# MLA layer: norm weights folded into the weight casts, and the norm epilogue issued one pass later

## The reference

```python
q_a  = x @ q_a_w.T                                  # 1536 wide
q    = rmsnorm(q_a, q_a_ln_w) @ q_b_w.T             # 16 heads of 128 + 64
ckv_full = x @ kv_a_w.T                             # 512 + 64 wide
kv   = rmsnorm(ckv_full[..., :512], kv_a_ln_w) @ kv_b_w.T
# rotary embedding on the 64-wide parts, causal attention over 2048 keys, attn @ o_w.T
x = layernorm(x + attention)
x = layernorm(x + (silu((x @ gate_w.T) * gate_s) * ((x @ up_w.T) * up_s)) @ down_w.T * down_s)

def rmsnorm(x, w):
    var = mean(x * x, -1);  return w * (x * rsqrt(var + 1e-6))
```

## Time and profile before

| | us |
|---|---|
| two runs | 5514.85 and 5719.79, median 5617.32 |
| profiled execution | 5525.08 |
| its span, slowest core (core 0) | 5523.5 |
| the eight cores' spans | 5457.2 to 5523.5 |
| busy: TensorE, VectorE, ScalarE | 3832.7, 1938.4, 1574.5 |

### The profile page before, as it was taken

One profiled execution on the slowest core, in us unless ns is written; L12 is line 12 of the kernel. 1 busy time (PEld: TensorE's weight loads), 2 busy tenths in 40 slices (PEclk: granted clock), 3 DMA queues, 4 the chain that ended last, 5 costly groups with the idle time before them and its releaser, 6 DMA issues.

```text
span 5523.5 us, 67067 instructions; the slowest of 8 cores (5457.2 to 5523.5 us)
## 1 busy us (share of the span) xinstructions
PE 3832.7 (69%) x20050; PEld 1841.4 (33%) x20400; DVE 1938.4 (35%) x4074; ACT 1574.5 (29%) x3152; POOL 327.9 (6%) x581
## 2 busy tenths in 40 slices
PE   0466657666666666666365679885998599859986
PEld 0222323223333333333122234342434244424443
DVE  2333222544444444444223233323332333233323
ACT  0000000025545454555200033222332233223322
POOL 0000000000000000000000011111111011111111
PEclk9877778878778887788677789997999899989998
DMA  4100022000000000000501079876887588658975
GB/s 127 57 31 31 20 71 67 16 12 9 5 9 5 11 5 9 5 5 1 152 31 38 23 232 279 255 249 196 277 271 244 187 277 281 230 187 268 279 247 183
DMA packets 207570, 674.50 MB, mean 122 GB/s; under 512 B 30016, under 2 KB 30528, under 8 KB 203136
## 3 DMA queue, kind: packets, MB, share of 16 engines
q1 hardware_dynamic: 120816, 341.68, 19.4%
q0 software_dynamic: 78928, 310.68, 18.0%
q10 hardware_dynamic: 7488, 17.83, 1.1%
HBM read 653.05 MB, written 16.78 MB: 121 GB/s over the span
## 4 chain that ended last, share of the span: by engine, by line
PE 35%; DMA 32%; DVE 13%; issue 11%; ACT 8%; DVEq 1%; SPq 0%; ACTq 0%; POOL 0%; POOLq 0%
DMA stg_gp<-up_l 20%; PE pD L1134 6%; PE pPT L556 5%; DMA stg_gp<-down_c 5%; PE pOP L924 4%; PE pQA L417 3%; ACT Ebuf L829 3%; PE pO L778 3%; ACT PTsb L801 3%; DVE ubf L229 2%; PE pPT L794 2%; PE pS L741 2%; DVE stats L759 2%; DMA stage<-ow_l 1%; PE pS L752 1%
## 5 line engine op out<-in xcount | busy, mean ns | idle before, releaser
L1063 PE MATMUL pU<-OX,ubf 128*128 128x512 bf16 x2756 | 644.8, 384 | 131.2 <-DVE ubf L229 127.0
L1054 PE MATMUL pG<-OX,gbf 128*128 128x512 bf16 x2760 | 641.2, 383 | 136.3 <-ACT gbf L226 133.5
L1134 PE MATMUL pD<-h_fm,dbf 128*128 128x512 bf16 x2756 | 625.5, 383 | 83.5 <-DVE dbf L229 75.8
L229 DVE CAST ubf<-stg_gp 128x1024 bf16<-128x1024 f32 x352 | 244.5, 695 | 871.7 <-DMA stg_gp<-up_l 854.9
L778 PE MATMUL pO<-PTsb,vtm 128*128 128x128 bf16 x2176 | 239.0, 238 | 312.3 <-ACT PTsb L801 305.8
L1063 PEld LDWEIGHTS pU<-OX,ubf 128*128 128x128 bf16 x2816 | 269.9, 99 | 496.3 <-issue 201.7
L1054 PEld LDWEIGHTS pG<-OX,gbf 128*128 128x128 bf16 x2816 | 277.5, 99 | 471.4 <-issue 145.7
L1134 PEld LDWEIGHTS pD<-h_fm,dbf 128*128 128x128 bf16 x2816 | 273.3, 99 | 423.3 <-issue 125.2
L801 ACT CAST PTsb<-pPT 128x512 bf16<-128x512 f32 (+3 forms) x640 | 313.5, 524 | 279.3 <-PE pPT L794 277.7
L829 ACT ACTIVATE Ebuf<-pS,stats 128x512 bf16<-128x512 f32 (+3 forms) x512 | 314.3, 621 | 208.7 <-DVE stats L820 207.6
L1076 ACT ACTIVATE sig<-pG,gates_sb 128x512 bf16<-128x512 f32 x176 | 120.9, 687 | 880.7 <-DVE tmid L1081 684.0
(11 more groups left out here) (135 smaller groups left out, 3756.1 us busy)
## 6 DMA issues: line engine op xcount, KB each, us to landing
stg_gp<-up_l POOLq DMA_DIRECT2D x352, 512.0 KB, 6.3
stg_sy<-gate_l SPq DMA_DIRECT2D x352, 512.0 KB, 6.3
stg_sy<-down_c SPq DMA_DIRECT2D x128, 512.0 KB, 6.0
stg_gp<-down_c POOLq DMA_DIRECT2D x128, 512.0 KB, 5.2
stg_sy<-down_c SPq DMA_DIRECT2D x64, 384.0 KB, 7.1
stg_gp<-down_c POOLq DMA_DIRECT2D x64, 384.0 KB, 4.4
stage<-x SPq DMA_DIRECT2D x64, 256.0 KB, 3.0
xst<-x POOLq DMA_DIRECT2D x16, 1024.0 KB, 5.7
```

Of the source, the lines that this page charges most:

```text
L229: e.tensor_copy(d[:, a:a + cc], tiles[i][:, 0:cc]), inc=cP)
L1054: P.op("tensor", lambda e, wi=wi, d=d, gc0=gc0: e.matmul(pG[wi][:], gbf[wi][:, d * 128:(d + 1) * 128], OX[:, d * S + gc0:d * S + gc0 + 512 ...
L1063: P.op("tensor", lambda e, wi=wi, d=d, gc0=gc0: e.matmul(pU[wi][:], ubf[wi][:, d * 128:(d + 1) * 128], OX[:, d * S + gc0:d * S + gc0 + 512 ...
L1134: P.op("tensor", lambda e, di=di, hh=hh, jj=jj, ii=ii: e.matmul(pD[di][:], dbf[hh][:, jj * 128:(jj + 1) * 128], h_fm[:, ii * 512:(ii + 1) ...
```

## The change

1. `qaln_rep` and `kvln_rep` are replaced by `qaln_cols` (128x12) and `kvln_cols` (128x4): column k holds the norm weights of rows 128k to 128k+127 of the weight matrix. The four staged loads and casts go; two small DMAs come, ahead of the tables, into tiles that need no cast.
2. The norm weights are multiplied onto the weights as these are cast. In stage A2 the 36 casts on VectorE become `tensor_scalar_mul` and the 36 on ScalarE become `activation` with function Copy and a scale of one value for each partition. In the heads each of the 32 `kvw3` casts becomes four multiplies of 128x128, as each block has its own column of weights.
3. In the epilogue the two VectorE operations that made `rq_tm` and `ckv_tm` (L448, L466) become Copy activations on ScalarE with the root as scale. Both sums of squares come first, then both means, both reciprocals, both roots, both copies.
4. The epilogue of pass t-1 is emitted in pass t, behind the x transposes and their evictions (L397) and behind the four casts of the next x chunk (L405), and ahead of `emit_a1_tr`. `emit_a1_tr` also waits on TensorE for the two copies.

```diff
-        def cast_stage(slot, ld, dst_ap, cols, eng="vector"):
+        def cast_stage(slot, ld, dst_ap, cols, eng="vector", scale=None):
...
+                P.op(eng, lambda e, i=slot, d=dst_ap, c=cols, s=scale:
+                     e.tensor_scalar_mul(d, stage[i][:, 0:c], s), inc=cW)
...
+                                 e.activation(d[:, a:a + cc], tiles[i][:, 0:cc],
+                                              AF.Copy, scale=sc), inc=cP)
...
+        P.op("sync", lambda e: e.dma_start(out=qln_c[:], in_=qaln_cols_in), inc=dC0, k=16)
+        P.op("sync", lambda e: e.dma_start(out=kln_c[:], in_=kvln_cols_in), inc=dC0, k=16)
...
-                load_cast(qaln_rep, qaln_sb, 0, QL)
-                load_cast(kvln_rep, kvln_sb, 0, LAT)
...
+                def emit_a1_epi(pi, pt, pmm):
+                    nonlocal pqa_free, pckv_free, pkpe_free
+                    P.w("scalar", sAct, sAct.n)
+                    P.w("scalar", tMM, pmm)
+                    P.op("scalar", lambda e: e.activation(
+                        junk[:, 0:QL], pQA[:], AF.Square,
+                        accum_out=stats[:, 0:1]), inc=sAct)
+                    sq_qa = sAct.n
+                    P.op("scalar", lambda e: e.activation(
+                        junk[:, 1536:1536 + LAT], pCKV[:], AF.Square,
+                        accum_out=stats[:, 3:4]), inc=sAct)
+                    sq_ckv = sAct.n
+                    P.w("vector", sAct, sq_qa)
+                    P.op("vector", lambda e: e.tensor_scalar(
+                        stats[:, 1:2], stats[:, 0:1], rql[:], EPS_RMS,
+                        op0=ALU.mult, op1=ALU.add), inc=vStat)
+                    P.w("vector", sAct, sq_ckv)
+                    P.op("vector", lambda e: e.tensor_scalar(
+                        stats[:, 4:5], stats[:, 3:4], 1.0 / LAT, EPS_RMS,
+                        op0=ALU.mult, op1=ALU.add), inc=vStat)
+                    P.w("vector", vStat, vStat.n)
+                    P.op("vector", lambda e: e.reciprocal(stats[:, 1:2], stats[:, 1:2]), inc=vStat)
+                    P.op("vector", lambda e: e.reciprocal(stats[:, 4:5], stats[:, 4:5]), inc=vStat)
+                    P.w("scalar", vStat, vStat.n)
+                    P.op("scalar", lambda e: e.activation(
+                        stats[:, 2:3], stats[:, 1:2], AF.Sqrt), inc=sAct)
+                    P.op("scalar", lambda e: e.activation(
+                        stats[:, 5:6], stats[:, 4:5], AF.Sqrt), inc=sAct)
+                    P.w("scalar", sAct, sAct.n)
+                    P.op("scalar", lambda e, pi=pi: e.activation(
+                        rq_tm[pi][:], pQA[:], AF.Copy,
+                        scale=stats[:, 2:3]), inc=sAct)
+                    pqa_free = (sAct, sAct.n)
+                    P.op("scalar", lambda e, pi=pi: e.activation(
+                        ckv_tm[pi][:], pCKV[:], AF.Copy,
+                        scale=stats[:, 5:6]), inc=sAct)
+                    pckv_free = (sAct, sAct.n)
+                    P.w("vector", dC1, tm_ld)
+                    P.w("vector", tMM, pmm)
+                    P.op("vector", lambda e: e.tensor_copy(kpe_sc[:], pKPE[:]), inc=vE)
+                    pkpe_free = (vE, vE.n)
+                    P.w("vector", vE, vE.n)
+                    P.op("vector", lambda e, pt=pt: e.tensor_mul(
+                        kpe_r1[:], kpe_sc[:], cos_tm[:, pt * ROPE:(pt + 1) * ROPE]), inc=vE)
+                    swap_ap = bass.AP(kpe_sc, 32, [[ROPE, 128], [-32, 2], [1, 32]])
+                    P.op("vector", lambda e, pt=pt, sw=swap_ap: e.tensor_tensor(
+                        kpe_r2[:].rearrange("p (a b) -> p a b", a=2), sw,
+                        sins_tm[:, pt * ROPE:(pt + 1) * ROPE].rearrange("p (a b) -> p a b", a=2),
+                        ALU.mult), inc=vE)
+                    P.w("vector", vE, vE.n)
+                    P.op("vector", lambda e: e.tensor_add(
+                        kpe_bf[:], kpe_r1[:], kpe_r2[:]), inc=vE)
+                    return vE.n
...
                 def emit_a1_tr(pi, pt, pkpe_done):
                     P.w("tensor", vE, pkpe_done)
+                    P.wf("tensor", pqa_free)
+                    P.wf("tensor", pckv_free)
...
                     if pend_epi is not None:
-                        emit_a1_tr(*pend_epi)
+                        kd = emit_a1_epi(*pend_epi)
+                        emit_a1_tr(pend_epi[0], pend_epi[1], kd)
...
-                    kpe_done = vE.n
-                    pend_epi = (i, t, kpe_done)
+                    pend_epi = (i, t, a1_mm)
...
+                            load_cast(src[grp, k], qbw_bf, slots[k] * 512, 512,
+                                      scale=qln_c[:, k:k + 1])
...
+                def kv_load(src, dst):
+                    sl, ld = stage_load(src, LAT)
+                    P.w("vector", dWs[sl], ld)
+                    P.w("vector", dC0, ln_cols_ld)
+                    for l in range(LATC):
+                        P.op("vector", lambda e, sl=sl, dst=dst, l=l: e.tensor_scalar_mul(
+                            dst[:, l * 128:(l + 1) * 128],
+                            stage[sl][:, l * 128:(l + 1) * 128],
+                            kln_c[:, l:l + 1]), inc=cW)
+                    stage_free[sl] = (cW, cW.n)
```

More of the change, by code:

```diff
@@ L181, in stage_load, with load_cast @@
             return i, dWs[i].n
-        def cast_stage(slot, ld, dst_ap, cols, eng="vector"):
+        def cast_stage(slot, ld, dst_ap, cols, eng="vector", scale=None):
             P.w(eng, dWs[slot], ld)
             if eng == "scalar":
-                P.op(eng, lambda e, i=slot, d=dst_ap, c=cols:
-                     e.copy(d, stage[i][:, 0:c]), inc=cS)
+                if scale is None:
+                    P.op(eng, lambda e, i=slot, d=dst_ap, c=cols:
+                         e.copy(d, stage[i][:, 0:c]), inc=cS)
+                else:
+                    P.op(eng, lambda e, i=slot, d=dst_ap, c=cols, s=scale:
+                         e.activation(d, stage[i][:, 0:c], AF.Copy, scale=s), inc=cS)
                 stage_free[slot] = (cS, cS.n)
                 return cS.n
-            P.op(eng, lambda e, i=slot, d=dst_ap, c=cols:
-                 e.tensor_copy(d, stage[i][:, 0:c]), inc=cW)
+            if scale is None:
+                P.op(eng, lambda e, i=slot, d=dst_ap, c=cols:
+                     e.tensor_copy(d, stage[i][:, 0:c]), inc=cW)
+            else:
+                P.op(eng, lambda e, i=slot, d=dst_ap, c=cols, s=scale:
+                     e.tensor_scalar_mul(d, stage[i][:, 0:c], s), inc=cW)
             stage_free[slot] = (cW, cW.n)
             return cW.n
-        def load_cast(src_ap, dst_tile, dst_c0, cols, eng="vector"):
+        def load_cast(src_ap, dst_tile, dst_c0, cols, eng="vector", scale=None):
             done = 0
@@ L201, in load_cast @@
                 done = cast_stage(sl, ld, dst_tile[:, dst_c0 + c0:dst_c0 + c0 + cc],
-                                  cc, eng)
+                                  cc, eng, scale)
                 c0 += cc
@@ L210, in mk_path, with lc @@
             st = {"free": [None] * nslots, "i": 0}
-            def lc(src_ap, dst_tile, dst_c0, cols):
+            def lc(src_ap, dst_tile, dst_c0, cols, scale=None):
                 done = None
@@ L431, in build_program @@
                     x0_free[i] = (tMM, a1_mm)
[L432 to L467, removed]
-                        op0=ALU.mult, op1=ALU.mult), inc=vE)
@@ L541, in q_group @@
                         if k % 2 == 0:
+                            P.w("vector", dC0, ln_cols_ld)
                             P.wf("vector", slot_free[slots[k]])
[L543 removed]
+                            load_cast(src[grp, k], qbw_bf, slots[k] * 512, 512,
+                                      scale=qln_c[:, k:k + 1])
                         else:
+                            P.w("scalar", dC0, ln_cols_ld)
                             P.wf("scalar", slot_free[slots[k]])
[L546 removed]
+                            w_cp = lc_a2(src[grp, k], qbw_bf, slots[k] * 512, 512,
+                                         scale=qln_c[:, k:k + 1])
                     w_ready = cW.n
```

65 lines of the change are left out of this document (29 added, 36 removed).

## The result

| | before | changed |
|---|---|---|
| all runs made side by side, median, us | 5665.25 (15 runs) | 5566.84 (16 runs) |
| lowest | 5510.81 | 5446.07 |
| profiled execution | 5525.08 | 5503.52 |
| ratio, with its 95% interval | | 0.9899 [0.9858, 0.9939] |

The changed kernel is 1.0% faster (0.6 to 1.4%), some 56 us of 5525. The two medians lie some 150 and 90 us above the runs that the ratio compares, because in over half of these executions (10 of 17 of the changed kernel) the cores of one die show a lower granted clock, 0.78 to 0.84 against 0.86, and the ratio leaves those out.

What follows compares the result with a forecast made beforehand. It took VectorE's single queue between products in stage A1, x load's round trip included, as the bound. Terms -38.5 - 1.7 - 6.0 + 1 + 4.8 = -40.4 us from 5525.1 gave 5485 us, range 5450 to 5530.

Steps and rivals of the forecast that it cites:

- the term for the spread between executions: Whole kernel: the slowest core's time alone was said to move by some 10 us between executions; used for the range.
- The gap of a pass: Stage A1, between one product's end and the next one's start: 2.6 us less in 15 gaps, 38.5 us (28 to 42).
- The rebuilt pass: Stage A1: one pass retimed station by station with the change, from product end at 427.24 to next product at 441.9.
- The clock: Stage A1 product: low granted clock in its first 5.3 us; bounds nothing to 37 us gain, counted as nothing.
- rises sooner: Rival in stage A1: TensorE's clock rises earlier in the product; full gain 5448 us, half 5466; chance 0.12.
- The start: Kernel start: tables issued from 2.9 instead of 8.87 us, so all later SyncE work moves 6.0 us earlier.
- Behind the last pass: End of stage A1, with no x load: the epilogue reaches the transposes at 700.3 instead of 701.98, 1.7 us less.
- A2: Stage A2: scaled casts cost 2.2 us more on VectorE, about nothing on ScalarE; +1 us taken (-1 to +3).
- The heads: Heads: four multiplies replace each cast; 16 on the path at 0.3 us each, +4.8 us (0 to 19).
- on which everything of that head waits: Heads: the values' multiplies run directly ahead of the head's first maximum and delay the whole head; 0.3 us each.
- No table was loaded: Rival: ScalarE reloads its function table around the copies; one load on the path 5505 us, both 5526; chances shared with others.
- The gap didn't stay: Rival in stage A1: evictions and squares slow each other, 2.8 us more per pass, 5523 us; 0.05 shared with double table loads.

Runs made afterwards that it cites:

- e3: Changed kernel with one plain 128x512 cast instead of four multiplies for each of the 32 head weights; heads 1457.3 us against 1457.9.
- e1: Kernel before with only the epilogue moved one pass later, behind the x evictions and casts; ratio to the kernel before 0.9949, pass 33.0 us on die 1.
- e2: Changed kernel with the epilogue back behind its own product, all else as changed; ratio 0.9880, pass 30.47 us.
- e4: Changed kernel with the next x chunk's four casts moved behind the evictions of the transposes; ratio 0.9839, pass 27.25 us on six cores.
- e7: Changed kernel with four stage buffers in place of two up to the end of stage A1; one run, 5429.76 us, pass 27.33 us.
- e5: Changed kernel with the epilogue back behind its own product and the x casts behind the transposes' evictions; ratio 0.9756, pass 26.10 us.
- e8: Changed kernel with epilogue back behind its own product, x casts behind the transposes' evictions, and four stage buffers; ratio 0.9712, pass 26.30 us.

## Why the prediction held, and where it failed

I forecast 5485 us, 5450 to 5530, and the median of all runs is 5566.84. **The step that failed is the last one, from the sum to the range: the term for the spread between executions, put at "some 10 us".** The runs showed in its place a spread of 314 us: the sixteen of the changed kernel go from 5446.07 to 5760.32, ten of them above 5530, and the fifteen of the kernel before from 5510.81 to 5825.83. The sum was made against the profiled execution, which lay by the lower of the two runs shown, and these two were 205 us apart already. By the median of the two I had 5577, only 10 us from the result, but that is luck: the median of the kernel before came out 48 us higher with fifteen runs. A range for a median of such runs would have had to reach as far as the 5665 of the kernel before, whatever the change.

The step of 40.4 us that the sum gives stands beside 56 (34 to 78) by the ratio and 43.2 by the two profiles. The seven runs on which the ratio rests, from 5446.07 to 5503.52 (the profiled one), have 5473.62 in the middle. So the sum was sound, in part by luck: its terms for the gap and for the clock were off in opposite directions.

The terms, as far as the profiles part them:

- **The gap of a pass**: forecast 2.6 us, measured 2.3 over the passes (1.8 in the two shown, 16.9 to 15.1). The rebuilt pass met nearly every station: evictions 0.56 behind the transposes (0.54 forecast), 2.60 for them (2.80), statistics 0.69 (0.7), roots 0.38 (0.4), copies and release 2.37 (2.15), to the product 3.77 (3.98, of which 0.4 is the missing record). Only the casts were 4.71 instead of 4.13, with a wait for x of 2.98 instead of 2.43 us. I had taken that wait from a single pass, and a short one: over all cores and passes with an x load the waits come to 3.0 us a pass before, where that pass has 2.6. In the changed kernel they come to 3.25, so that "the wait doesn't shrink" was right and it grew by 0.2.
- **The clock**, counted at nothing, gave the 0.7 us by which the product got shorter; in the two products shown half of 5.3 - 3.7 is 0.8. That is 11 us, and the rival "rises sooner" came true to a third of its bound of 37. With 34.6 by the gaps the passes gave 45.6 us for 38.5.
- **The start**: the tables were issued at 2.92, for 2.9 forecast, which is the whole 6 us on SyncE:

```profile
1.98 0.42 SPq L267 DMA_DIRECT2D qln_c<-qaln_cols  x1
2.45 0.43 SPq L268 DMA_DIRECT2D kln_c<-kvln_cols  x1
2.92 0.43 SPq L327 DMA_DIRECT2D cos_tm_sb<-cos_tm  x1
```

  By the mean over the cores the first sum of squares came 4.2 us sooner, by core from 9.2 sooner to 2.3 later. The 80 slices behind it scatter by more than the term.
- **Behind the last pass**: 1.5 for 1.7.
- **A2**: -1.7 for +1, within its scatter over the cores. The prices, by form and line, as the earlier trace rows:

```profile
L239 ACT ACTIVATE qbw_bf<-stg_a,qln_c 128x512 bf16<-128x512 f32 x36 | 26.0, 721 | 332.5 <-DMA stg_a<-qbn_g 183.0 <-DMA stg_a<-qbp_g 149.5
...
L199 DVE TENSOR_SCALAR qbw_bf<-stage,qln_c 128x512 bf16<-128x512 f32 x36 | 17.0, 485 | 38.6 <-DMA stage<-qbn_g 26.1 <-DMA stage<-qbp_g 12.0
```

  VectorE's multiply took the 485 ns of the row that I chose. ScalarE's activation took 721 and not "about nothing" over the 617 of the cast; the Square that I took as nearest has a constant scale. It cost no time that can be seen.
- **The heads**: forecast +4.8, measured 3.9 between the two profiles. But e3 gives the casts back and gains nothing, so the 3.9 is mostly scatter; by the means over all kernels and the stretch ahead of the heads the term is nearer 2 us. The four multiplies in one row:

```profile
L684 DVE TENSOR_SCALAR kvw<-stage,kln_c 128x128 bf16<-128x128 f32 x128 | 27.7, 281 | 3.7 <-DMA stage<-kvbk_l 3.4 <-PE pS L792 0.3
```

  The timeline at a head's first maximum, in the changed kernel (core 2) and in e3 (core 4):

```profile
1310.66 0.52 DVE L737 CAST vtm<-pPT 128x128 bf16<-128x128 f32 x2 [0.41 <-PE pPT L730]
1311.13 0.87 DVE L684 TENSOR_SCALAR kvw<-stage,kln_c 128x128 bf16<-128x128 f32 x4
1311.92 0.28 DVE L799 TENSOR_REDUCE stats<-pS 128x1 f32<-128x128 f32 x1
```

```profile
1320.28 0.51 DVE L737 CAST vtm<-pPT 128x128 bf16<-128x128 f32 x2 [0.41 <-PE pPT L730]
1320.71 0.42 DVE L196 CAST kvw<-stage 128x512 bf16<-128x512 f32 x1
1321.05 0.28 DVE L799 TENSOR_REDUCE stats<-pS 128x1 f32<-128x128 f32 x1
```

  Four take 0.87 from first to last, more than my 0.69 and under the 1.02 without overlap. From the end of the last eviction to the maximum it is 0.74 us with the multiplies (0.73 to 0.75 at 13 of this core's 16 heads) and 0.26 with the cast (0.24 to 0.26 at 14), so the delay is there at nearly each head, and at 0.5 it is larger than the 0.3 that I took. That it doesn't add up to some 7 us over the heads points to slack further on in the head; where, wasn't tried. So the step "on which everything of that head waits" doesn't hold by these runs, and that 4.8 lies near 3.9 is luck.

**The rivals.** No table was loaded: the one load before the heads is still that of the start, 1.28 us. That agrees with the rule of the Trainium skill, "ScalarE: Activation LUTs", on table sets, that copy is in each set. The gap didn't stay.

**The reason behind the sum was half wrong, though the sum was right.** I put the gain down to work ahead of the evictions turning into "0.5 of waiting for a transpose and 4.0 of statistics and copies". That is an account of the chain in one arrangement. It doesn't tell what each part of the change is worth, and e1 and e2 do: taking the two products off VectorE and doing the statistics in pairs gives 3.3 us a pass where it stands, the move gives 0.8 alone and nothing on top. How much of the 3.3 is the products and how much the pairs, no run here parts; the two products are 1.82 and 0.75 us in the earlier trace rows. I should have rebuilt the pass for each part by itself; the rows for it were the same.

## What to carry to other kernels

When a chain runs through one engine's queue, moving a piece to another place in that queue shifts it; only what leaves the queue, or stands beside the long work of another engine, is gained. Look at what else stands in the chain before rearranging: here a DMA round trip, asked for too late because there were only two buffers, was worth more than the change (4.2 us a pass by moving the casts, against 3.0; and with four buffers 52 us at the start besides). And a forecast for a measured median needs the spread of the runs shown, not the spread over the cores of one profile.

## What the runs showed of the hardware

**A Copy with a scale per partition took ScalarE about 90 ns longer than a Square.** The Copy activations with such a scale took 1541 and 680 ns in the changed kernel (1.54 and 0.68 in the pass above), the Squares of the same shapes with no such operand 1451 and 589. The two differ in their function too, and no run here has a Copy without the scale on these shapes. The difference agrees with the Trainium skill, "ScalarE: Activation LUTs", the section on what a table load costs, which gives about 93 ns for each such operand and the same for the overlap of neighbours. An estimate by that page's formula for an activation with one such operand, 2.17 us for both copies, is nearer to the measured 2.12 (411.97 to 414.09) than my 2.0 from the nearest rows.

**The slowest core was made in the FFN, which the change doesn't touch.** The changed kernel's cores:

```profile
core 0: 5409.5 us, clock 0.864
...
core 2: 5501.6 us, clock 0.864
```

Core 2 reached the FFN at 3145.2 us, 7.8 behind core 0, and needed 2311.2 us for it, against 2226.8. The line view of the casts of one weight over that stage, core 0, then core 2 (busy us, mean ns, idle before and its releaser):

```profile
L244 DVE CAST ubf<-stg_gp 128x1024 bf16<-128x1024 f32 x350 | 243.6, 696 | 828.8 <-DMA stg_gp<-up_l 802.7 <-PE pU L1103 26.1
```

```profile
L244 DVE CAST ubf<-stg_gp 128x1024 bf16<-128x1024 f32 x350 | 243.3, 695 | 914.4 <-DMA stg_gp<-up_l 893.5 <-PE pU L1103 12.3 <-PE pG L1094 8.6
```

The casts are equal, and the wait for their DMA is 893.5 against 802.7 us. In e4 and e7 too two or three cores needed 2280 to 2330 us for the FFN and the rest 2224 to 2250; in e5 and e8 none did. So the slowest core of one execution can tell of 80 us that lie in a stage whose code the change doesn't touch, and the mean over the cores by stage is the better reading of a change in one stage. What makes one core's transfers late wasn't tried.
